# Moving preparation work earlier in a linear-attention layer with a routed feed-forward, and swapping two GpSimd operations

## The chip, the cores and the metric

The kernel runs on one core of one Trainium2 chip. The metric is the device time of one execution in microseconds. Engines are called TensorE (PE in the rows), VectorE (DVE), ScalarE (ACT), GpSimd (POOL) and SyncE (SP, which issues the DMAs).

## The reference

One transformer layer on 8192 tokens of width 512, float32. The six modulation vectors sa, ca, ga, sb, cb, gb come from `silu(c) @ wmod`; ga and gb are kept away from zero.

```python
h = layernorm(x) * (1 + ca) + sa
q, k = elu(h @ Wq.T + bq) + 1, elu(h @ Wk.T + bk) + 1     # 16 heads of 32
v = h @ Wv.T + bv
KV = sum over tokens of k (x) v;  Z = 1 / (q . sum(k) + 1e-6)
x = x + ga * ((q @ KV * Z) @ Wo.T + bo)
h = layernorm(x) * (1 + cb) + sb
V = h @ fWv.T + fbv                                        # value mix
s = ln(V @ Wg.T + bg) + sigmoid(alpha) * ln(norms of the probes Wp @ V)
w = softmax of the two best of 8 experts
x = x + gb * (V + sum over experts of w_e * (silu(V @ W1_e.T + b1_e) @ W2_e.T + b2_e))
```

## The kernel before

The work has two phases with one pass over the tokens each. The first is `sweep_tiles` over T = 64 tiles of 128 tokens. A tile i is normalised (xn), turned (xT), multiplied by Wk and Wq; k of the tile is multiplied with xn into four PSUM banks that gather over all tiles (the sum over tokens), and q goes to DRAM. The second phase is `sweep_pairs` over 32 pairs of tiles, and reads q back. Between them a few products build the matrix G from the sums.

Every matmul operand is split in a high and a low part (`_hi`, `_lo`, float32r), and `three` (L1471) makes three products of them: 12 matmuls of 128x512 for each of the three products of a tile, 36 in a step. In TensorE's step i (L1578) stand k(i), the product of k(i-1) with xn(i-1), and q(i). Each waits for what the other engines made: k(i) for xT_hi from ScalarE (L774), its last third for xT_lo from VectorE (L970); the second product for k_lo from VectorE and xn_lo from GpSimd.

VectorE's step i (L1180) runs in this order: zq of the tile before (L1184, tile qf in the rows), statistics of tile i+2 (L940 to L948), in steps 1 to 16 one `modulation` (L1191), qf (L1195), zk (L1201), xn of tile i+2 (L958), the turn of tile i+1 (L964), kf (L1213, tile zk in the rows), xT_lo (L970), k_lo (L1221). `modulation(v, b)` multiplies one quarter of a 512x512 block of wmod by silu(c) and adds it into row v of mod2; v = 0 to 3 are ga, sb, cb, gb, four steps each. L1044 is the first quarter of each, L1047 the three others.

GpSimd's step i (L656): rstd of tile i+2 (L662), xn_lo of tile i+1 (L667, behind ScalarE's xn_hi, L780), and ks_acc (L672), which adds kf of tile i to the sum of k.

All weights are prepared on the chip, and this work is laid between the tiles by the table `PREP` (L50): step to two lists of jobs, the first run in front of xn of the step (on TensorE behind the k product), the second at the step's end. `prepare` (L1085 on VectorE, L1540 on TensorE, L753 on ScalarE) and `scaled` (L1062) run them. The jobs: bq; sb, gb, ga (TensorE sums a row of mod2 over the partitions, L1492 or L1504; for ga and gb ScalarE copies it to wtmp and VectorE makes the gate of it by `gate`, L1052; ga also multiplies bo_ga, L1113); cat0 to cat3 (VectorE turns a quarter of the router and expert weights and adds it into acc_c, L1097 to L1108); fv, u, bc, bfv, w2 (the products of the value mix with them); v, bv, o (attention's value and output weights). Semaphores keep them in order, and every engine meets the jobs in program order, so that a job that takes long on VectorE delays the tile work behind it.

Of the kernel before, what the change touches and what calls it, by code (L numbers as in the profile page):

```python
# [23 lines left out]
ALU = mybir.AluOpType  # L24
# [7 lines left out]
KB = D // P  # L32
# [14 lines left out]

PREP = {0: ["bq", ""], 13: ["sb", ""], 17: ["gb", ""], 19: ["", "cat0"], 20: ["", "cat1"], 21: ["", "cat2"],  # L50
# [4 lines left out]
PREP_STEPS = 57  # L55
MOD2_LOADS = {-1: 0, 1: 1, 6: 2, 9: 3}


def f32(ap):

    return ap.bitcast(F32)


def wait_count(eng, sem, n):

    if not isinstance(n, int) or n > 0:
        eng.wait_ge(sem, n)
# [14 lines left out]
def prep_job(i, n):  # L82

    return [j for j in PREP.get(i, [])[n:n + 1] if j]


def live(t, tiles):

    return not isinstance(t, int) or 0 <= t < tiles
# [7 lines left out]
def landed(t, slot):  # L97

    return (t - slot) * 8 + 16
# [12 lines left out]
def build(nc, x, Wq, bq, Wk, bk, Wv, bv, Wo, bo, fWv, fbv, Wg, bg, Wp, alpha, g_r, b_r, g_c, b_c,  # L112
          W1, b1, W2, b2, c, wmod, out):
    T = x.shape[1] // P
    assert T % 2 == 0 and T > PREP_STEPS
    J = T // 2
# [9 lines left out]
    with ctx:  # L126
        def sb(name, shape, dt=F32, stack=ctx):
            return stack.enter_context(nc.sbuf_tensor(name, shape, dt))

        def sem(name):  # L130
            return ctx.enter_context(nc.semaphore(name))
# [16 lines left out]
        ks_acc = sb("ks_acc", [P, D])  # L148
# [62 lines left out]
        kf = zk  # L211
# [121 lines left out]
        kf_done = sem("kf_done")  # L333
        kh_done = sem("kh_done")
        kl_done = sem("kl_done")
        ks_done = sem("ks_done")
# [94 lines left out]

        for step_jobs in PREP.values():
            JOBS += [j for j in step_jobs if j and j[0] != "v" and j[:3] != "cat"]
# [6 lines left out]

        SUMMED = {j: n for n, j in enumerate([j for step_jobs in PREP.values() for j in step_jobs
                                              if j[:3] == "cat" or j[:2] == "fv" or j[:1] in ("u", "v")])}

        W_TURNS = {j: n for n, j in enumerate([j for step_jobs in PREP.values() for j in step_jobs
                                               if j[:3] == "cat" or j[:2] == "w2" or j[:1] in ("o", "v")])}
# [41 lines left out]
        def quarters(row):  # L487

            return row.rearrange("p (j i d) -> p i j d", i=KB, j=KB)

        def natural(row):

            return row.rearrange("p (i j d) -> p i j d", i=KB, j=KB)
# [139 lines left out]
        def _(pool):  # L633
# [22 lines left out]
            def step(i, s):  # L656
                if -1 <= i <= 0:
                    pool.wait_ge(xn_done, i + 2)
                    nc.gpsimd.tensor_copy(quarters(xq[:, 1 - s, :]), natural(xn[:, 1 - s, :])).then_inc(xp_done, 1)
                if live(i + 2, T):  # L660
                    wait_count(pool, veps_done, i + 3)
                    nc.gpsimd.tensor_tensor(rstd[:, s:s + 1], veps[:, s:s + 1], neg_half[:, 0:1],  # L662
                                            ALU.pow).then_inc(rstd_done, 1)
                if live(i + 1, T):
                    pool.wait_ge(xnh_done, i + 2)
                    pool.wait_ge(xn_done, i + 2)
                    nc.gpsimd.tensor_tensor(quarters(xn_lo[:, 1 - s, :]), natural(xn[:, 1 - s, :]),  # L667
                                            quarters(f32(xn_hi[:, 1 - s, :])), ALU.subtract).then_inc(xnl_done, 1)
                if live(i, T):
                    pool.wait_ge(kf_done, i + 1)  # L670
                    wait_count(pool, ks_done, i)
                    nc.gpsimd.tensor_tensor(ks_acc[:], ks_acc[:], kf[:, s, :], ALU.add).then_inc(ks_done, 1)  # L672

            sweep_tiles(step, -2, T - 1)

            def biased_x(j):
# [247 lines left out]
        def _(dve):  # L924
# [13 lines left out]
            def statistics(i, s):  # L938
                dve.wait_ge(x_in[s], landed(i, s))
                nc.vector.bn_stats(stats[:, s, :], xin[:, s, :]).then_inc(stats_done, 1)  # L940
                dve.wait_ge(stats_done, i + 1)

            def mean_var(i, s):
                nc.vector.bn_aggr(mv[:, s, :], stats[:, s, :]).then_inc(mv_done, 1)

            def var_eps(i, s):
                dve.wait_ge(mv_done, i + 1)
                nc.vector.tensor_scalar(veps[:, s:s + 1], mv[:, s, 1:2], EPS, None, ALU.add).then_inc(veps_done, 1)  # L948
# [89 lines left out]
            ga, gb = mod2[:, GA, :], mod2[:, GB, :]  # L1038

            def modulation(v, b):  # L1040

                dve.wait_ge(wmv_in[v], 16)
                if b == 0:
                    ins = nc.vector.tensor_scalar(mod2[:, v, :], wm_in[:, v % 2, b, :], c_col[:, 2, b:b + 1], None, ALU.mult)  # L1044
                else:
                    dve.wait_ge(mod2_done, KB * v + b)
                    ins = nc.vector.scalar_tensor_tensor(out=mod2[:, v, :], in0=wm_in[:, v % 2, b, :],  # L1047
                                                         scalar=c_col[:, 2, b:b + 1], in1=mod2[:, v, :],
                                                         op0=ALU.mult, op1=ALU.add)
                ins.then_inc(mod2_done, 1)  # L1050
# [129 lines left out]
            def step(i, s):  # L1180
                if live(i - 1, T):
                    dve.wait_ge(q_psum, i)
                    wait_count(dve, q_out[1 - s], landed(i - 1, 1 - s) - 16)
                    nc.vector.tensor_tensor(zq[:, 1 - s, :], bank_q, bq_row[:], ALU.add).then_inc(zq_done, 1)  # L1184
                early_turn = i == 0
                ahead = live(i + 2, T)
                if ahead:
                    statistics(i + 2, s)
                    mean_var(i + 2, s)
                    var_eps(i + 2, s)  # L1190
                if 1 <= i <= 4 * KB:  # L1191
                    modulation((i - 1) // KB, (i - 1) % KB)
                if live(i - 1, T):
                    dve.wait_ge(eq_done, i)
                    nc.vector.scalar_tensor_tensor(out=qf[:, 1 - s, :], in0=zq[:, 1 - s, :], scalar=0.0,  # L1195
                                                   in1=exp_q[:, 1 - s, :], op0=ALU.max, op1=ALU.add).then_inc(qf_done, 1)
                if live(i, T):
                    dve.wait_ge(k_psum, i + 1)
                    wait_count(dve, kh_done, i - 1)
                    wait_count(dve, ks_done, i - 1)  # L1200
                    nc.vector.tensor_tensor(zk[:, s, :], bank_k, bk_row[:], ALU.add).then_inc(zk_done, 1)  # L1201
                if early_turn:
                    for b in range(KB):
                        low_q(b)
                    xT_low(i + 1, 1 - s)
                prepare(i, 0)
                if ahead:
                    normed(i + 2, s)
                if live(i + 1, T) and not early_turn:
                    turned_x(i + 1, 1 - s)  # L1210
                if live(i, T):
                    dve.wait_ge(ek_done, i + 1)
                    nc.vector.scalar_tensor_tensor(out=kf[:, s, :], in0=zk[:, s, :], scalar=0.0,  # L1213
                                                   in1=exp_k[:, s, :], op0=ALU.max, op1=ALU.add).then_inc(kf_done, 1)
                    scaled(i)
                    if live(i + 1, T) and not early_turn:
                        xT_low(i + 1, 1 - s)
                    dve.wait_ge(kf_done, i + 1)
                    dve.wait_ge(kh_done, i + 1)
                    wait_count(dve, m_done, i - 1)  # L1220
                    nc.vector.tensor_tensor(k_lo[:, s, :], kf[:, s, :], f32(k_hi[:, s, :]), ALU.subtract).then_inc(kl_done, 1)  # L1221
                prepare(i, 1)
                if i == 15:
                    bias_columns()
                if i == 35:
                    b2_and_value_bias()
                if isinstance(i, int) and i == PREP_STEPS - 1:
                    router_constants()

            sweep_tiles(step, 0, T)  # L1230


# [512 lines left out]
```

## Time and profile before

| | us |
|---|---|
| median of 3 runs | 1271.91 (1270.49 to 1272.03) |
| profiled execution | 1271.91 |
| its span, first to last instruction | 1270.2 |
| PE busy | 1224.7 (96%) |
| DVE busy | 997.0 (78%) |
| ACT busy | 538.0 (42%) |
| POOL busy | 547.8 (43%) |

Times in rows count from the start of the span. Busy time of an engine is the time in which an instruction of it runs, and an instruction that is held up by something inside the machine counts as running. TensorE's matmuls overlap: one of 128x512 is shown with 0.39 us and the next starts 0.23 us later. The table of the program's groups calls a tile by its name in the kernel without the buffer's number, so mod2 appears as mod and the gathered sums as ps.

### The profile page before, as it was taken

The page shows a single profiled execution, that of the slowest core. Times are in us where ns is not written, and L with a number is a line of the kernel's source. Part 1 is how long each engine was busy: PE and PEld are TensorE (multiplying, and loading weights), DVE is VectorE, ACT ScalarE, POOL GpSimd, SP SyncE. Part 2 cuts the span into 40 slices and gives each one's busy share as a digit, 9 for nine tenths or more (in the row PEclk, how much of TensorE's full clock was granted, in tenths as well). Part 3 has the DMA queues.
Part 4 walks back from the last instruction along what each step waited for, and adds up shares of the span by engine and source line. Part 5 has one row for each costly group of instructions (what it writes and reads, how often), then busy time and mean ns, then how long its engine had stood idle before and what let it go on. Part 6 is the DMA issues. An engine that isn't in the chain of part 4 may idle for free.

```text
span 1270.2 us, 18483 instructions
## 1 busy us (share of the span) xinstructions
PE 1224.7 (96%) x5742; PEld 999.4 (79%) x5742; DVE 997.0 (78%) x2275; ACT 538.0 (42%) x1117; POOL 547.8 (43%) x401
## 2 busy tenths in 40 slices
PE   8999999999999999998789999999999999999998
PEld 5788878788777788885678888788887888888887
DVE  5887788888889888877578777777877777778764
ACT  2454454545445554443334343433434334343431
POOL 1434433333334433433346464554645445364531
PEclk9999999999999999999899999999999999999999
DMA  8455534444334443432322221313223131322201
GB/s 214 157 174 178 162 122 144 145 137 126 108 105 127 133 133 108 125 116 75 83 67 67 84 92 58 100 55 96 73 78 99 51 100 59 92 84 66 84 17 51
DMA packets 131681, 131.64 MB, mean 104 GB/s; under 512 B 12328, under 2 KB 86480, under 8 KB 131584
## 3 DMA queue, kind: packets, MB, share of 16 engines
q1 hardware_dynamic: 131584, 130.47, 33.8%
q8 instruction: 46, 0.75, 0.3%
q14 instruction: 51, 0.42, 0.1%
HBM read 80.62 MB, written 49.81 MB: 103 GB/s over the span
## 4 chain that ended last, share of the span: by engine, by line
PE 65%; DVE 11%; POOL 11%; issue 6%; ACT 4%; DMA 1%; SPq 0%; POOLq 0%; DVEq 0%; ACTq 0%
PE ps L1475 20%; PE ps L1476 20%; PE ps L1480 20%; POOL xb L679 6%; POOL rrs L718 3%; PE ps L1662 2%; POOL rstd L711 2%; DVE x L1303 2%; DVE xT_lo L1310 1%; DVE marked L1393 1%; PE ps L1568 1%; ACT xn L879 1%; DVE zk L1201 1%; DMA wm_in<-in_L_wmod_dram 1%; DVE m L1386 1%
## 5 line engine op out<-in xcount | busy, mean ns | idle before, releaser
L705 POOL TENSOR_TENSOR cn<-c,half 128x16 f32<-128x16 f32 x32 | 104.2, 3257 | 281.5 <-DVE c L1338 281.5
L667 POOL TENSOR_TENSOR xn_lo<-xn,xn_hi 128x512 fp32r<-128x512 f32 x64 | 85.5, 1337 | 278.1 <-ACT xn_hi L780 278.1
L1475 PE MATMUL ps<-g_hi,qT_hi 128*128 128x512 f32 x256 | 104.8, 410 | 4.9 <-ACT qT_hi L843 4.9
L798 ACT ACTIVATE exp_q<-qf 128x512 f32<-128x512 f32 x64 | 40.5, 632 | 156.7 <-DVE qf L1184 156.7
L1475 PE MATMUL ps<-wk_hi,xT_hi 128*128 128x512 f32 x256 | 102.0, 398 | 2.4 <-ACT xT_hi L774 2.4
L1475 PE MATMUL ps<-wq_hi,xT_hi 128*128 128x512 f32 x256 | 102.4, 400 | 0.5 <-DVE wq_lo L1006 0.5
L1475 PE MATMUL ps<-v_hi,xT_hi 128*128 128x512 f32 x256 | 102.9, 402 | 0.0
L1475 PE MATMUL ps<-k_hi,xn_hi 128*128 128x512 f32 x256 | 102.3, 400 | 0.0
L1476 PE MATMUL ps<-g_lo,qT_hi 128*128 128x512 f32 x256 | 101.8, 398 | 0.0
L1476 PE MATMUL ps<-wq_lo,xT_hi 128*128 128x512 f32 x256 | 101.4, 396 | 0.0
L1476 PE MATMUL ps<-wk_lo,xT_hi 128*128 128x512 f32 x256 | 101.3, 396 | 0.0
L1476 PE MATMUL ps<-k_lo,xn_hi 128*128 128x512 f32 x256 | 100.7, 393 | 0.0
L1476 PE MATMUL ps<-v_lo,xT_hi 128*128 128x512 f32 x256 | 100.2, 391 | 0.0
L1480 PE MATMUL ps<-k_hi,xn_lo 128*128 128x512 f32 x256 | 100.1, 391 | 0.0
L836 ACT CAST xT_hi<-ps 128x512 fp32r<-128x512 f32 x64 | 37.5, 587 | 131.9 <-PE ps L1662 131.9
L672 POOL TENSOR_TENSOR ks_acc<-ks_acc,zk 128x512 f32<-128x512 f32 x64 | 88.0, 1376 | 4.6 <-DVE zk L1213 4.6
L679 POOL TENSOR_TENSOR xb<-xin,bo_ga 128x1024 f32<-128x1024 f32 x32 | 77.8, 2431 | 9.5 <-DMA xin<-_attn_hidden_states_dram 9.3
L1475 PE MATMUL ps<-c_hi,xT_hi 128*128 128x328 f32 x256 | 80.7, 324 | 0.0
L697 POOL TENSOR_TENSOR qks<-q_in,ks_q 128x1024 f32<-128x1024 f32 x32 | 76.9, 2403 | 8.4 <-DMA q_in<-q_scratch 8.4
L1476 PE MATMUL ps<-c_lo,xT_hi 128*128 128x328 f32 x256 | 77.9, 315 | 0.0
L805 ACT ACTIVATE exp_k<-zk 128x512 f32<-128x512 f32 x64 | 40.6, 634 | 87.9 <-DVE zk L1201 87.8
L662 POOL TENSOR_TENSOR rstd<-veps,neg_half 128x1 f32<-128x1 f32 x64 | 44.7, 698 | 73.5 <-DVE veps L948 72.7
(240 smaller groups left out, 3292.5 us busy)
## 6 DMA issues: line engine op xcount, KB each, us to landing
xin<-_attn_hidden_states_dram SPq DMA_DIRECT2D x64, 256.0 KB, 3.1
q_scratch<-qf SPq DMA_DIRECT2D x64, 256.0 KB, 3.3
xin<-_attn_hidden_states_dram SPq DMA_DIRECT2D x32, 512.0 KB, 4.1
q_in<-q_scratch SPq DMA_DIRECT2D x128, 128.0 KB, 2.9
out_dram<-qf SPq DMA_DIRECT2D x64, 256.0 KB, 2.0
xn_scratch<-xn SPq DMA_DIRECT2D x62, 256.0 KB, 2.1
xq<-xn_scratch SPq DMA_DIRECT2D x248, 64.0 KB, 2.4
wm_in<-in_L_wmod_dram SPq DMA_DIRECT2D x4, 1024.0 KB, 5.6
```

Of the source, the lines that this page charges most:

```text
L662: nc.gpsimd.tensor_tensor(rstd[:, s:s + 1], veps[:, s:s + 1], neg_half[:, 0:1], ALU.pow).then_inc(rstd_done, 1)
L667: nc.gpsimd.tensor_tensor(quarters(xn_lo[:, 1 - s, :]), natural(xn[:, 1 - s, :]), quarters(f32(xn_hi[:, 1 - s, :])), ALU.subtract).then_in ...
L672: nc.gpsimd.tensor_tensor(ks_acc[:], ks_acc[:], kf[:, s, :], ALU.add).then_inc(ks_done, 1)
L679: nc.gpsimd.tensor_tensor(xb[:], xin[:], bo_ga[:].unsqueeze(1).to_broadcast([P, 2, D]), ALU.add).then_inc(xb_done, 1)
L697: nc.gpsimd.tensor_tensor(qks[:].rearrange("p h (g f) -> p (h g) f", f=P), q_of(j).rearrange("p (n f) -> p n f", f=P), ks_q[:].unsqueeze(1 ...
L705: nc.gpsimd.tensor_tensor(cn[:].rearrange("p h e -> p (h e)"), c2[:].rearrange("p h e -> p (h e)"), half[:], ALU.pow).then_inc(cn_done, 1)
L718: nc.gpsimd.tensor_tensor(rrs[:].rearrange("p h k -> p (h k)"), rve[:], neg_half[:, 0:4], ALU.pow).then_inc(rrs_done, 1)
L798: nc.scalar.activation(exp_q[:, 1 - s, :], zq[:, 1 - s, :], ACT.Relu, scale=-1.0).then_inc(rq_done, 1)
L805: nc.scalar.activation(exp_k[:, s, :], zk[:, s, :], ACT.Relu, scale=-1.0).then_inc(rk_done, 1)
L1475: nc.tensor.matmul(dst, ah, bh, start=start and n == 0, stop=False)
L1476: nc.tensor.matmul(dst, ah, bl, start=False, stop=False)
L1480: last = nc.tensor.matmul(dst, al_, bh, start=False, stop=stop and n == len(parts) - 1)
```

## The change

Three things are changed. The `PREP` table puts ga at step 6 instead of 50, the jobs cat0 to cat3 two steps earlier (17 to 20, with gb at 18 instead of 17), and all that follows two to five steps earlier; `router_constants` thereby runs at step 51 instead of 56, and `b2_and_value_bias` at 24 instead of 35. On VectorE the `modulation` of steps 1 to 16 stands behind k_lo instead of behind the statistics. On GpSimd ks_acc(i) stands ahead of xn_lo(i+1).

```diff
-PREP = {0: ["bq", ""], 13: ["sb", ""], 17: ["gb", ""], 19: ["", "cat0"], 20: ["", "cat1"], 21: ["", "cat2"],
-        22: ["", "cat3"], 24: ["", "fv0"], 25: ["u0", ""], 27: ["", "fv1"], ...
+PREP = {0: ["bq", ""], 6: ["", "ga"], 13: ["sb", ""], 17: ["", "cat0"], 18: ["gb", "cat1"], 19: ["", "cat2"],
+        20: ["", "cat3"], 22: ["", "fv0"], 23: ["u0", ""], 25: ["", "fv1"], ...
...
@@ GpSimd
+                if live(i, T):
+                    pool.wait_ge(kf_done, i + 1)
+                    wait_count(pool, ks_done, i)
+                    nc.gpsimd.tensor_tensor(ks_acc[:], ks_acc[:], kf[:, s, :], ALU.add).then_inc(ks_done, 1)
                 if live(i + 1, T):
                     pool.wait_ge(xnh_done, i + 2)
                     pool.wait_ge(xn_done, i + 2)
                     nc.gpsimd.tensor_tensor(quarters(xn_lo[:, 1 - s, :]), natural(xn[:, 1 - s, :]),
                                             quarters(f32(xn_hi[:, 1 - s, :])), ALU.subtract).then_inc(xnl_done, 1)
-                if live(i, T):
-                    pool.wait_ge(kf_done, i + 1)
-                    wait_count(pool, ks_done, i)
-                    nc.gpsimd.tensor_tensor(ks_acc[:], ks_acc[:], kf[:, s, :], ALU.add).then_inc(ks_done, 1)
@@ VectorE
                     var_eps(i + 2, s)
-                if 1 <= i <= 4 * KB:
-                    modulation((i - 1) // KB, (i - 1) % KB)
                 if live(i - 1, T):
...
                     nc.vector.tensor_tensor(k_lo[:, s, :], kf[:, s, :], f32(k_hi[:, s, :]), ALU.subtract).then_inc(kl_done, 1)
+                if 1 <= i <= 4 * KB:
+                    modulation((i - 1) // KB, (i - 1) % KB)
                 prepare(i, 1)
                 if i == 15:
                     bias_columns()
-                if i == 35:
+                if i == 24:
                     b2_and_value_bias()
```

The order on the engines shows the change at three places. In the changed kernel kf, k_lo, qf and zk have the lines L1211, L1219, L1193 and L1199, and ks_acc and xn_lo on GpSimd L667 and L671.

GpSimd before, at the first tiles: xq is a copy for the first two tiles alone.

```order
L662 TENSOR_TENSOR rstd<-veps,neg_half 128x1
L667 TENSOR_TENSOR xn_lo<-xn,xn_hi 128x4x4x32
L672 TENSOR_TENSOR ks_acc<-ks_acc,zk 128x512
L662 TENSOR_TENSOR rstd<-veps,neg_half 128x1
L667 TENSOR_TENSOR xn_lo<-xn,xn_hi 128x4x4x32
```

GpSimd of the changed kernel, at the same place.

```order
L662 TENSOR_TENSOR rstd<-veps,neg_half 128x1
L667 TENSOR_TENSOR ks_acc<-ks_acc,zk 128x512
L671 TENSOR_TENSOR xn_lo<-xn,xn_hi 128x4x4x32
L662 TENSOR_TENSOR rstd<-veps,neg_half 128x1
L667 TENSOR_TENSOR ks_acc<-ks_acc,zk 128x512
```

The two operations have changed places in each step.

VectorE before, step 6, from veps to the first operation of step 7: mod is the modulation's accumulator.

```order
L948 TENSOR_SCALAR veps<-mv 128x1
L1047 SCALAR_TENSOR_TENSOR mod<-wm_in,c_col,mod 128x512
L1195 SCALAR_TENSOR_TENSOR qf<-qf,exp_q 128x512
L1201 TENSOR_TENSOR zk<-ps,bk_row 128x512
L958 TENSOR_SCALAR xn<-xin,mv,rstd 128x512
L964 STREAM_TRANSPOSE ps<-xq 128x4x4x32
L1213 SCALAR_TENSOR_TENSOR zk<-zk,exp_k 128x512
L970 TENSOR_TENSOR xT_lo<-ps,xT_hi 128x512
L1221 TENSOR_TENSOR k_lo<-zk,k_hi 128x512
L1184 TENSOR_TENSOR qf<-ps,bq_row 128x512
```

VectorE of the changed kernel, step 6 from xn on, again to the first operation of step 7.

```order
L958 TENSOR_SCALAR xn<-xin,mv,rstd 128x512
L964 STREAM_TRANSPOSE ps<-xq 128x4x4x32
L1211 SCALAR_TENSOR_TENSOR zk<-zk,exp_k 128x512
L970 TENSOR_TENSOR xT_lo<-ps,xT_hi 128x512
L1219 TENSOR_TENSOR k_lo<-zk,k_hi 128x512
L1047 SCALAR_TENSOR_TENSOR mod<-wm_in,c_col,mod 128x512
L1056 TENSOR_SCALAR wtmp<-wtmp 128x512
L1057 TENSOR_SCALAR wtmp<-wtmp 128x512
L1058 TENSOR_TENSOR wtmp<-wtmp 128x512
L1059 SCALAR_TENSOR_TENSOR mod<-wtmp 128x512
L1113 TENSOR_TENSOR bo_ga<-bo_ga,mod 128x512
L1184 TENSOR_TENSOR qf<-ps,bq_row 128x512
```

The modulation has moved from the front to behind k_lo, and the five operations of the gate ga have come in behind it.

VectorE of the changed kernel, step 18, from zk to the middle of cat1. Before, the four operations of the gate stood at this place of step 17, and no job stood behind k_lo in steps 17 and 18.

```order
L1199 TENSOR_TENSOR zk<-ps,bk_row 128x512
L1056 TENSOR_SCALAR wtmp<-wtmp 128x512
L1057 TENSOR_SCALAR wtmp<-wtmp 128x512
L1058 TENSOR_TENSOR wtmp<-wtmp 128x512
L1059 SCALAR_TENSOR_TENSOR mod<-wtmp 128x512
L958 TENSOR_SCALAR xn<-xin,mv,rstd 128x512
L964 STREAM_TRANSPOSE ps<-xq 128x4x4x32
L1211 SCALAR_TENSOR_TENSOR zk<-zk,exp_k 128x512
L970 TENSOR_TENSOR xT_lo<-ps,xT_hi 128x512
L1219 TENSOR_TENSOR k_lo<-zk,k_hi 128x512
L1100 STREAM_TRANSPOSE catT<-raw_cat 128x352
L1103 TENSOR_REDUCE small<-catT 128x1
```

Gate and cat job now stand in one step, with cat0 in the step ahead of it and cat2 and cat3 in the two behind.

## Rows read from the trace of the kernel before

**Rows 1.** The page: span, and busy time of TensorE with its share and instructions.
```profile
span 1270.2 us, 18483 instructions
PE 1224.7 (96%) x5742; PEld 999.4 (79%) x5742; DVE 997.0 (78%) x2275; ACT 538.0 (42%) x1117; POOL 547.8 (43%) x401
```
**Rows 2.** Chain of waits in order of time: start us, us, what.
```profile
62.24 0.93 PE ps L1480 x4
70.61 0.93 PE ps L1480 x4
```
**Rows 3.** Waits of TensorE's weight loads, first phase: us in total, times, longest.
```profile
PEld ps L1475 <- ACT xT_hi L774: 4.7, 6, 1.3
```
**Rows 4.** Timeline, first matmul of steps: start, us, what [idle before <-releaser].
```profile
216.23 0.39 PE L1475 MATMUL ps<-wk_hi,xT_hi 128*128 128x512 f32 x1
...
225.05 0.50 PE L1475 MATMUL ps<-wk_hi,xT_hi 128*128 128x512 f32 x1 [0.29 <-ACT xT_hi L774]
...
234.54 0.50 PE L1475 MATMUL ps<-wk_hi,xT_hi 128*128 128x512 f32 x1 [0.89 <-ACT xT_hi L774]
...
372.03 0.39 PE L1475 MATMUL ps<-wk_hi,xT_hi 128*128 128x512 f32 x1
...
424.18 0.39 PE L1475 MATMUL ps<-wk_hi,xT_hi 128*128 128x512 f32 x1
```
**Rows 5.** Timeline, VectorE from one L1184 to the next around cat2, and GpSimd.
```profile
210.33 0.68 DVE L1184 TENSOR_TENSOR qf<-ps,bq_row 128x512 f32<-128x512 f32 x1
...
215.03 0.69 DVE L1213 SCALAR_TENSOR_TENSOR zk<-zk,exp_k 128x512 f32<-128x512 f32 x1 [0.27 <-ACT exp_k L807]
...
216.47 0.69 DVE L1221 TENSOR_TENSOR k_lo<-zk,k_hi 128x512 fp32r<-128x512 f32 x1
...
218.39 1.55 DVE L997 SCALAR_TENSOR_TENSOR acc_c<-catT,col_turn,acc_c 128x328 f32<-128x328 f32 x1
219.86 0.68 DVE L1184 TENSOR_TENSOR qf<-ps,bq_row 128x512 f32<-128x512 f32 x1
...
218.28 1.29 POOL L672 TENSOR_TENSOR ks_acc<-ks_acc,zk 128x512 f32<-128x512 f32 x1
```
**Rows 6.** Timeline, VectorE and GpSimd in the last tile.
```profile
581.56 0.69 DVE L1213 SCALAR_TENSOR_TENSOR zk<-zk,exp_k 128x512 f32<-128x512 f32 x1 [1.36 <-ACT exp_k L807]
583.00 1.18 DVE L1221 TENSOR_TENSOR k_lo<-zk,k_hi 128x512 fp32r<-128x512 f32 x1 [0.74 <-ACT k_hi L813]
...
582.33 1.29 POOL L672 TENSOR_TENSOR ks_acc<-ks_acc,zk 128x512 f32<-128x512 f32 x1 [4.61 <-DVE zk L1213]
```
**Rows 7.** Timeline, GpSimd and VectorE in step 27.
```profile
269.36 1.30 POOL L667 TENSOR_TENSOR xn_lo<-xn,xn_hi 128x512 fp32r<-128x512 f32 x1 [4.47 <-ACT xn_hi L780]
270.61 1.74 POOL L672 TENSOR_TENSOR ks_acc<-ks_acc,zk 128x512 f32<-128x512 f32 x1
...
269.83 1.37 DVE L1221 TENSOR_TENSOR k_lo<-zk,k_hi 128x512 fp32r<-128x512 f32 x1
271.13 1.78 DVE L1081 TENSOR_TENSOR v_lo<-wtmp,v_hi 128x512 fp32r<-128x512 f32 x1
```
**Rows 8.** The modulation's two lines: count, ns min/median/max, first and last start.
```profile
L1044 DVE TENSOR_SCALAR mod<-wm_in,c_col x4: 479/479/1164, 40.3 to 140.1; 128x512 f32<-128x512 f32 x4
...
L1047 DVE SCALAR_TENSOR_TENSOR mod<-wm_in,c_col,mod x12: 751/752/1043, 48.1 to 167.1; 128x512 f32<-128x512 f32 x12
```
**Rows 9.** Timeline, VectorE: gate gb in step 17, bo_ga in step 50.
```profile
178.00 0.43 DVE L1056 TENSOR_SCALAR wtmp<-wtmp 128x512 f32<-128x512 f32 x1 [0.79 <-ACT wtmp L759]
...
180.38 0.55 DVE L958 TENSOR_SCALAR xn<-xin,mv,rstd 128x512 f32<-128x512 f32 x1
...
478.46 0.69 DVE L1113 TENSOR_TENSOR bo_ga<-bo_ga,mod 128x512 f32<-128x512 f32 x1
```
**Rows 10.** TensorE's line L1504 (job sb): count, ns, first and last start.
```profile
L1504 PE MATMUL ps<-ones,mod x16: 166/250/250, 141.1 to 142.7; 128*128 128x1 f32 x16
```
**Rows 11.** Sums of a stretch: busy time of each engine, granted clock, DMA.
```profile
603.00:610.00 7.00, 3.83 (x9) 3.08 (x10) 6.90 (x8) 1.33 (x3) 1.33 (x1) 0.55 0.50 150
```

More of the change, by code:

```diff
@@ L46 @@
 TAKEN = -3.3e38
-PREP = {0: ["bq", ""], 13: ["sb", ""], 17: ["gb", ""], 19: ["", "cat0"], 20: ["", "cat1"], 21: ["", "cat2"],
[4 rows of a table removed]
-PREP_STEPS = 57
+PREP = {0: ["bq", ""], 6: ["", "ga"], 13: ["sb", ""], 17: ["", "cat0"], 18: ["gb", "cat1"], 19: ["", "cat2"],
[4 rows of a table added]
+PREP_STEPS = 52
 MOD2_LOADS = {-1: 0, 1: 1, 6: 2, 9: 3}
```

8 rows, old and new, of the table PREP are left out of this document.

## The prediction

> **What bounds the kernel now.** I read the page first, then the chain of waits, what TensorE waits for, and last the rows of VectorE, GpSimd and TensorE beside each other. TensorE is busy 96% of the span [rows 1]. In the first phase (64 tiles) its chain repeats the same block of L1480 every 8.37 us [rows 2]: that is 36 matmuls of one tile back to back, and no step can be shorter. So an edit of this phase pays or costs only by how long TensorE is left without input. It waits for one thing there: xT_hi, six times, 4.7 us of its weight loads [rows 3]. The first wk_hi matmul of steps 22, 24, 39 and 45 starts at 216.23, 234.54, 372.03 and 424.18 [rows 4]. Two steps take 18.31 instead of 16.74 (1.57 lost), six take 52.15 instead of 50.22 (1.93 lost). That is 3.5 us of stall in the whole phase, and more is not to be had by moving this work.
>
> Why xT_hi is late: VectorE falls behind. Call lag the time from TensorE's start of a step to VectorE's L1184 in it. L1184 at 219.86 [rows 5] and TensorE's next start at 225.05, ended by xT_hi [rows 4], are 5.19 apart. So TensorE's step lasts 8.37 plus its own extra work, or lag + 5.19 if that is longer: the limit is a lag of 3.18. Lag grows by VectorE's own period minus TensorE's step, and can't fall under about 0.34.
>
> VectorE's period is where the change acts. In the cat step L1184 follows L1184 after 9.53 us (210.33, 219.86) [rows 5]. The last piece is L997, 1.55 us for 328 columns, which ends 0.37 after GpSimd's ks_acc (218.28 + 1.29). That is a block, not work: VectorE waits while GpSimd's instruction runs.
>
> **Who blocks whom.** Two places show it in full. In the last tile, where no xn_lo comes first, ks_acc starts 0.08 after kf (581.56 + 0.69) and k_lo, issued at 583.00, takes 1.18, ending 0.55 after ks_acc [rows 6]. In step 27 three turns follow each other: GpSimd xn_lo 269.36 to 270.66, VectorE k_lo until 271.20, GpSimd ks_acc stretched to 1.74 until 272.35, VectorE v_lo until 272.91 [rows 7]. When both have an instruction waiting, they alternate. From GpSimd's first start to the end of VectorE's second blocked instruction it is 3.55 us.
>
> The Trainium skill (SBUF — State Buffer, section "Who interferes with whom") has the rule that speaks against this change: an instruction of VectorE with two SBUF inputs and one of GpSimd that reads SBUF exclude each other for the whole instruction, and who starts first goes first. The trace agrees, with 1.18 for k_lo; the rule says nothing of the order when both queue, for which rows 7 stand. If the two only shared bandwidth, k_lo would be stretched in part and the forecast would come out near the first rival.
>
> **The swap on GpSimd.** Every tile: before, ks_acc came after xn_lo, so k_lo was issued before GpSimd had anything running. Now ks_acc starts at kf + 0.08, and k_lo, issued 0.7 later, waits. From rows 5, kf ends 5.39 after L1184 (215.72 - 210.33). So k_lo ends at 5.39 + 0.08 + 1.29 + 0.55 = 7.31, where it ended at 6.83 (216.47 + 0.69), and the next L1184 starts 0.08 earlier than that end. Ordinary period when lagging: 7.23 instead of 6.75. Cost 0.48 per step; hidden below 8.37, but lag is worked off more slowly. In return GpSimd's pair is over at 5.39 + 0.08 + 3.0 = 8.47 (3.0 from GpSimd's two instructions of [rows 7]), so a cat step ends its last piece at about 9.0 instead of 9.53: four times 0.5 gained. v_lo, w_lo and b2st gain likewise, mostly in steps that TensorE covers anyway.
>
> **The modulations.** Sixteen of them (four L1044, twelve L1047), steps 1 to 16, move from behind veps to behind k_lo. At the old place most took 0.48 and 0.75 [rows 8], part of it in the time in which VectorE waited for exp_q anyway. At the new place GpSimd's xn_lo stands in the queue when k_lo ends, takes the turn, and the modulation is the second blocked instruction of the pattern of rows 7. Period: 5.39 + 0.08 + 3.55 - 0.07 = 8.95 for L1047, and 8.68 for L1044 (0.27 shorter). Both are over 8.37. The bounds of one such step: 7.23 + 0.67 = 7.90 if it takes the pair before xn_lo, 8.95 by the nearest rows, 9.2 if GpSimd kept the pair for both of its instructions. I take 8.95, since rows 7 have this very queue.
>
> **The gate ga, step 50 to 6.** The TensorE sum costs the same (0.85 of its own work in the step) at either place. On VectorE four instructions take 2.38 (178.00 to 180.38) and bo_ga 0.73 [rows 9], 3.11 in all, 3.2 with the wait between. At step 50 it was hidden; now it lands on steps with no slack.
>
> **The sum, steps 1 to 16.** VectorE: 12 x 8.95 + 4 x 8.68 + 3.2 (gate) + 0.35 (sb_col, cb1_col) + 0.48 (bias_columns) = 146.1. TensorE without stall: 16 x 8.37 + 0.85 (ga) + 1.75 (sb: its 16 narrow matmuls, the last at 1.6 behind the first [rows 10]) = 136.5. The lag at step 1 is 1.3 (before it was 0.8, and k_lo is 0.5 later) and at step 17 it stands at 8.95 - 5.19 = 3.76, so 2.5 of the difference are absorbed. Stall: 146.1 - 136.5 - 2.5 = 7.1 us, from step 5 on, with the largest piece in step 7, behind the gate. The last modulation of step 12 is also awaited by sb in step 13: about 1.1 us, part of the 7.1.
>
> **Steps 17 to 21** (cat0, gb + cat1, cat2, cat3, nothing). VectorE 8.85 + 11.4 + 9.0 + 9.0 + 7.23 = 45.5, where 11.4 is 9.0 and the gate's 2.4. TensorE 5 x 8.37 + 0.86 (gb) = 42.7. Lag goes from 3.76 to 7.23 - 5.19 = 2.04, which gives back 1.7 as stall: 45.5 - 42.7 + 1.7 = 4.5 us. Before, the same four cat steps cost 1.7, as they began with no lag and gb stood two steps ahead of them.
>
> **Steps 22 to 63.** fv and u: TensorE's own transposes and matmuls in these steps cover VectorE, before as after. bfv behind bc: VectorE about 12.3 against 9.21, lag 3.45, stall 0.3 (0.7 before). w2: period 9.2 instead of 10.5, lag at most 2.9, none (1.2 before). v: 9.0 instead of 8.4, for acc_v now meets xn_lo; lag climbs to 3.7 at step 45, where bv's 0.9 on TensorE covers it. Stall here 0.3.
>
> Total stall 7.1 + 4.5 + 0.3 = 11.9, less the 3.5 of before: +8.4. Executions: the span was 1270.2 [rows 1] and the profiled time 1271.91, so 1.7 lie around it, and that time is also the median of the runs shown. The second phase runs the same instructions and I give it nothing. **1271.9 + 8.4 = 1280.3 us.**
>
> **Rivals.**
> 1. VectorE keeps the pair. If L1047 gets in directly after k_lo, its period is 7.90, steps 1 to 16 have no lag but for the gate, and the cats start from nearly none: lag 0.8, 3.0, 3.6, 3.8 and a stall of 1.4 in all. 1271.9 - 3.5 + 1.4 = 1269.8; with the gate of step 6 blocked once, near 1271. For it: the earlier end of GpSimd's pair, seen as 1.5 us in L997. Against it: ks_acc's 1.74 and v_lo's 1.78 in rows 7, which alternate. It decides at a period of 8.37.
> 2. GpSimd keeps the pair for both of its instructions. Then k_lo ends at 8.6 and even an ordinary step takes 8.5, over 8.37: another 4 us in steps 1 to 16 and 4 or more behind. About 1288. Against it: k_lo got in between xn_lo and ks_acc in rows 7.
> 3. TensorE's clock falls in the holes. Behind a hole of 3 us between the phases the granted clock is 0.55 over 603 to 610 [rows 11], that is mostly the level of 1.2 GHz. The hole of step 7, 3.3 us in two pieces, is the largest here. Some eight microseconds of matmuls at half speed would add 4 us, so 1284. Against it: the stalls of 0.3 and 0.9 in rows 4 left the clock at full speed. The Trainium skill (TensorE: Matmul & The Clock Gate, "What's actually happening") says that the clock follows how busy the array has lately been; here the holes after step 7 are 0.6 in 9, so I don't expect it.
>
> **How the numbers follow.** Forecast 0.74, its own range 1277 to 1283.5 (a period of 8.8 to 9.1 for the modulation steps is 2.4 us either way). Rival 1: 0.13, most of it faster, some within the bound. Rival 2: 0.04. Rival 3: 0.09. A measurement of this kernel can tell about 0.2% (2.5 us) from no change; the three runs lie within 1.5 us. So faster 0.09, same 0.08, slower 0.83. The range is 1275 to 1285: it leaves out most of rival 1 and rival 2.
>
> **What would show it.** Right: k_lo about 1.2 us in nearly all of 64 tiles; the modulations 1.7 or more, each ending 0.55 behind xn_lo; xn_lo stretched to 1.74; TensorE waiting for xT_hi in steps 5 to 12 by 0.3 to 0.6 and in step 7 by over 3; L1184 to L1184 8.95 there; L997 at about 0.5. Wrong: modulations of 0.75 behind k_lo, or steps 8 to 12 at 8.37; or a granted clock under 1.00 between 80 and 260 us, which would be rival 3.

## The result and the profile after

| | before | changed |
|---|---|---|
| median, us | 1271.97 (4 runs) | 1280.55 (4 runs, 1279.32 to 1280.94) |
| profiled execution | 1271.91 | 1278.65 |
| its span | 1270.2 | 1276.9 |

The ratio is 1.0064 with a 95% interval of 1.0052 to 1.0078, so the changed kernel is slower, clear of the noise: by 8.6 us between the two medians above, by 8.1 us by the ratio, which takes in more executions than these four. A later series of the same kernel gave 1280.39 and 1.0068 (1.0056 to 1.0081).

First the steps of the first phase, as [rows 4] show them for before. Timeline of TensorE in the changed kernel, first wk_hi matmul of steps 1, 7, 8, 9, 10, 17, 22 and 63 (start us, us, what, idle before and what ended it):

```profile
38.07 0.40 PE L1475 MATMUL ps<-wk_hi,xT_hi 128*128 128x512 f32 x1
...
89.36 0.39 PE L1475 MATMUL ps<-wk_hi,xT_hi 128*128 128x512 f32 x1
...
100.76 0.51 PE L1475 MATMUL ps<-wk_hi,xT_hi 128*128 128x512 f32 x1 [1.39 <-ACT xT_hi L774]
...
109.70 0.50 PE L1475 MATMUL ps<-wk_hi,xT_hi 128*128 128x512 f32 x1 [0.33 <-ACT xT_hi L774]
...
118.64 0.50 PE L1475 MATMUL ps<-wk_hi,xT_hi 128*128 128x512 f32 x1 [0.32 <-ACT xT_hi L774]
...
181.64 0.39 PE L1475 MATMUL ps<-wk_hi,xT_hi 128*128 128x512 f32 x1
...
227.96 0.50 PE L1475 MATMUL ps<-wk_hi,xT_hi 128*128 128x512 f32 x1 [0.39 <-ACT xT_hi L774]
...
584.45 0.39 PE L1475 MATMUL ps<-wk_hi,xT_hi 128*128 128x512 f32 x1
```

Timeline of TensorE in the kernel before, the first wk_hi matmul of steps 1, 17 and 63 (that of 22 is in [rows 4]):

```profile
37.93 0.39 PE L1475 MATMUL ps<-wk_hi,xT_hi 128*128 128x512 f32 x1
...
173.53 0.39 PE L1475 MATMUL ps<-wk_hi,xT_hi 128*128 128x512 f32 x1
...
576.51 0.39 PE L1475 MATMUL ps<-wk_hi,xT_hi 128*128 128x512 f32 x1
```

| stretch | before | changed | difference | forecast |
|---|---|---|---|---|
| steps 1 to 16 | 135.60 | 143.57 | +7.97, of it 0.85 the sum of ga and 7.1 stall | 7.1 stall |
| steps 17 to 21 | 42.70 | 46.32 | +3.6 stall | 4.5 |
| steps 22 to 62 | 360.28 | 356.49 | -3.79, of it -0.85 ga and -2.9 stall | -3.2 |
| together | 538.58 | 546.38 | +7.8 | +8.4 |

In the table, stall is the time that TensorE stood without input, and ga the 0.85 us of its own work that moved with the gate. The last column is the prediction's. Steps 8 and 9 last 8.94 each (100.76, 109.70, 118.64), where a step of before takes 8.37 [rows 2], and step 7 takes 11.40.

Waits of TensorE's weight loads in the first phase of the changed kernel (us in total, times, longest); before it was 4.7 us in six waits [rows 3]:

```profile
PEld ps L1475 <- ACT xT_hi L774: 10.8, 13, 2.1
PEld ps L1475 <- DVE qf L1184: 1.6, 1, 1.6
```

The second row is a wait that before did not have: q of step 7 needs its PSUM bank, and VectorE frees it with L1184, late behind the gate.

Then the cause. Timeline of VectorE and of GpSimd in step 10 of the changed kernel (L1211 is kf, L1219 k_lo, GpSimd's L667 ks_acc, L671 xn_lo):

```profile
126.84 0.69 DVE L1211 SCALAR_TENSOR_TENSOR zk<-zk,exp_k 128x512 f32<-128x512 f32 x1 [0.27 <-ACT exp_k L807]
127.45 0.69 DVE L970 TENSOR_TENSOR xT_lo<-ps,xT_hi 128x512 fp32r<-128x512 f32 x1
128.28 1.17 DVE L1219 TENSOR_TENSOR k_lo<-zk,k_hi 128x512 fp32r<-128x512 f32 x1
129.38 1.78 DVE L1047 SCALAR_TENSOR_TENSOR mod<-wm_in,c_col,mod 128x512 f32<-128x512 f32 x1
131.08 0.68 DVE L1184 TENSOR_TENSOR qf<-ps,bq_row 128x512 f32<-128x512 f32 x1
...
127.61 1.29 POOL L667 TENSOR_TENSOR ks_acc<-ks_acc,zk 128x512 f32<-128x512 f32 x1 [3.15 <-DVE zk L1211]
128.86 1.75 POOL L671 TENSOR_TENSOR xn_lo<-xn,xn_hi 128x512 fp32r<-128x512 f32 x1
```

This is the queue of [rows 7] with other names: ks_acc until 128.90, k_lo until 129.45, xn_lo until 130.61, the modulation until 131.16. Each of the two VectorE instructions ends 0.55 behind the GpSimd instruction that blocked it. xT_lo, with one input in PSUM, runs 0.69 beside ks_acc. All instances of the lines (count, ns min/median/max, first and last start) in the changed kernel; [rows 8] showed the modulations at 479 and 752:

```profile
L1047 DVE SCALAR_TENSOR_TENSOR mod<-wm_in,c_col,mod x12: 1767/1776/1782, 55.3 to 183.2; 128x512 f32<-128x512 f32 x12
...
L1044 DVE TENSOR_SCALAR mod<-wm_in,c_col x4: 1509/1514/1519, 46.6 to 156.2; 128x512 f32<-128x512 f32 x4
...
L1219 DVE TENSOR_TENSOR k_lo<-zk,k_hi x64: 743/1184/1455, 38.3 to 590.9; 128x512 fp32r<-128x512 f32 x64
...
L671 POOL TENSOR_TENSOR xn_lo<-xn,xn_hi x64: 1267/1745/1767, 18.1 to 583.2; 128x512 fp32r<-128x512 f32 x64
```

Not one of the sixteen modulations escapes the queue, and nearly every k_lo is stretched (1.18 in the middle of 64).

### The profile page after: what moved, and what is told of

The parts are those of the page before. It is cut to its first block, busy times and chain, and to the rows that moved or that the text cites. A ratio compares the mean times of both kernels' runs of the same rounds, so it can differ in the third digit from the quotient of the medians.

```text
span 1276.9 us, 18483 instructions
## 1 busy us (share of the span) xinstructions
PE 1225.7 (96%) x5742; PEld 997.7 (78%) x5742; DVE 1025.5 (80%) x2275; ACT 537.6 (42%) x1117; POOL 558.1 (44%) x401
## 4 chain that ended last, share of the span: by engine, by line
PE 58%; DVE 15%; POOL 11%; issue 7%; ACT 7%; DMA 1%; SPq 0%; DVEq 0%; POOLq 0%; ACTq 0%
PE ps L1475 18%; PE ps L1476 18%; PE ps L1480 17%; POOL xb L679 6%; POOL rrs L718 3%; PE ps L1662 2%; POOL rstd L711 2%; DVE x L1303 2%; DVE mod L1047 2%; DVE xT_lo L1310 1%; DVE zk L1199 1%; DVE zk L1211 1%; DVE qf L1184 1%; ACT exp_k L805 1%; ACT exp_q L798 1%
## 5 line engine op out<-in xcount | busy, mean ns | idle before, releaser
L667 POOL TENSOR_TENSOR ks_acc<-ks_acc,zk 128x512 f32<-128x512 f32 x64 | 83.1, 1299 | 219.1 <-DVE zk L1211 219.1
L671 POOL TENSOR_TENSOR xn_lo<-xn,xn_hi 128x512 fp32r<-128x512 f32 x64 | 109.6, 1712 | 0.0
L662 POOL TENSOR_TENSOR rstd<-veps,neg_half 128x1 f32<-128x1 f32 x64 | 35.3, 551 | 135.3 <-DVE veps L948 135.3
L1219 DVE TENSOR_TENSOR k_lo<-zk,k_hi 128x512 fp32r<-128x512 f32 x64 | 75.6, 1182 | 8.5 <-ACT k_hi L813 1.7
```

## The experiments

The whole time of an execution also varies in stretches that no edit touches (see the last section), so for each kernel the length of the first phase, from the start of step 1 to that of step 63, stands beside the median. That length is from the one profiled execution. The ratios are against executions of the kernel before on the same chip in the same series, with medians of 1271.56 (e1 to e4), 1271.42 (e5 to e7) and 1271.17 (e8, e9).

| kernel | table | modulation | GpSimd | first phase | median | ratio, 95% interval |
|---|---|---|---|---|---|---|
| before | old | front | xn_lo first | 538.6 | 1271.97 | |
| changed | new | behind k_lo | ks_acc first | 546.4 | 1280.55 | 1.0064 (1.0052 to 1.0078) |
| e1 | new | front | ks_acc first | 536.8 | 1271.49 | 0.9995 (0.9987 to 1.0004) |
| e2 | new | behind k_lo | xn_lo first | 542.9 | 1278.28 | 1.0053 (1.0040 to 1.0067) |
| e3 | new | front | xn_lo first | 540.2 | 1274.79 | 1.0026 (1.0018 to 1.0035) |
| e4 | old | front | ks_acc first | 535.8 | 1269.02 | 0.9979 (0.9970 to 0.9987) |
| e5 | old | behind k_lo | xn_lo first | 538.6 | 1271.34 | 0.9995 (0.9984 to 1.0006) |
| e6 | new | behind k_lo | ks_acc, then memset | 536.0 | 1270.29 | 0.9987 (0.9977 to 0.9997) |
| e7 | new, ga at 46 | behind k_lo | ks_acc first | 547.9 | 1280.96 | 1.0073 (1.0052 to 1.0093) |
| e8 | new, sb at 14 | behind k_lo | ks_acc first | 546.4 | 1279.79 | 1.0067 (1.0053 to 1.0080) |
| e9 | the changed kernel again | | | 547.3 | 1280.39 | 1.0068 (1.0056 to 1.0081) |

Against the medians of before, the first phase accounts for the whole time to within 0.8 us in the changed kernel, e4, e5, e7, e8 and e9. The medians of e1, e2, e3 and e6 are 1.5 to 2.4 us higher than their first phase would make them. Why is not shown.

The single edits and their sum are worth a look. In the first phase the table alone costs 1.6 (e3), the modulations' place alone nothing (e5), and GpSimd's order alone gives back 2.8 (e4); together they cost 7.8. The old table with both new orders was not run.

**e1: the modulations back in front.**

```diff
                     var_eps(i + 2, s)
+                if 1 <= i <= 4 * KB:
+                    modulation((i - 1) // KB, (i - 1) % KB)
...
-                if 1 <= i <= 4 * KB:
-                    modulation((i - 1) // KB, (i - 1) % KB)
                 prepare(i, 1)
```

> The changed kernel with the modulations of steps 1 to 16 back behind the statistics; the table and GpSimd's new order stay. Theory of the turns (VectorE's second blocked instruction behind k_lo makes a step 8.95 long): the modulation is now outside the queue, a modulation step is under 7.7 on VectorE, TensorE loses nothing in steps 8 to 13, step 7 has no stall (lag 0.3 + 11 - 9.2 = 2.1, limit 3.18), the cats start from no lag and stall 1.1 in steps 20 and 21, bfv 0.3. Stall of the first phase about 1.5 instead of 11.3, so the time is 1270 to 1271, 2 below the kernel before. Rival (the table's density costs the time: ga on step 6, gb beside cat1): the stalls of steps 7 and 18 stay, about 5 us, and the time is 1276 or more.

The first phase shrinks by 9.6 us to 536.8, 1.8 under before: steps 1 to 16 take 136.47 (before plus the 0.85 of ga), step 7 has 8.37, and steps 17 to 21 take 43.82, with the 1.1 expected. The rival is refuted. The median fell by 9.1, to that of before on the same chip (1271.56); the 2 us under it that were expected are not in the medians. They are in the profiles, 1269.87 against 1271.91, but e1's profiled execution is the fastest of its eleven. The modulation in front takes 0.75 in all twelve:

```profile
L1047 DVE SCALAR_TENSOR_TENSOR mod<-wm_in,c_col,mod x12: 750/751/753, 46.7 to 166.5; 128x512 f32<-128x512 f32 x12
```

**e2: GpSimd's old order.**

```diff
-                if live(i, T):
-                    nc.gpsimd.tensor_tensor(ks_acc[:], ks_acc[:], kf[:, s, :], ALU.add).then_inc(ks_done, 1)
                 if live(i + 1, T):
...
+                if live(i, T):
+                    nc.gpsimd.tensor_tensor(ks_acc[:], ks_acc[:], kf[:, s, :], ALU.add).then_inc(ks_done, 1)
```

> The changed kernel with GpSimd's old order (xn_lo, then ks_acc); table and modulations behind k_lo stay. Theory of the turns: k_lo is issued before xn_lo and takes 0.69, the modulation is blocked once, by xn_lo alone, and VectorE's modulation step is 8.45 instead of 8.95, so TensorE loses 0.1 per step in 8 to 12. But each cat step is 9.5 again (L997 at 1.55 behind ks_acc) and the ordinary one 7.0, so steps 17 to 21 stall about 5 and w2 and bfv about 2.5. About 1277 to 1279. Rival (GpSimd's swap alone is the harm, by k_lo at 1.18 in each tile): the time falls to about 1272.

The median of 1278.28 is within the expected range, but 2.4 us of its distance from before lie outside the first phase. The modulation step on VectorE is 8.45 (L1184 to L1184), steps 8 to 12 of TensorE last 8.36 to 8.47, steps 1 to 16 138.59. Cats and gate cost 3.7 in steps 17 to 21, where about 5 was expected, and w2 stalls again as before. Step 7 still loses 1.3. The modulation of step 6 is blocked behind xn_lo, and with GpSimd's old order the first instruction of the gate is blocked behind ks_acc (1.51, where it takes 0.41 in the changed kernel):

```profile
87.56 1.78 DVE L1047 SCALAR_TENSOR_TENSOR mod<-wm_in,c_col,mod 128x512 f32<-128x512 f32 x1
89.27 1.51 DVE L1056 TENSOR_SCALAR wtmp<-wtmp 128x512 f32<-128x512 f32 x1
...
87.47 1.33 POOL L667 TENSOR_TENSOR xn_lo<-xn,xn_hi 128x512 fp32r<-128x512 f32 x1 [4.33 <-ACT xn_hi L780]
88.77 1.73 POOL L672 TENSOR_TENSOR ks_acc<-ks_acc,zk 128x512 f32<-128x512 f32 x1
```

**e3: the table alone.** Both edits of e1 and e2.

> The new table alone: modulations in front and GpSimd's old order. Theory of the turns: steps 1 to 16 as before but for the gate behind step 6, 12.1 on VectorE, lag 3.2 against a limit of 3.2, no more than 0.3 of stall; cats of 9.5 beside the gate gb stall 4.5 in steps 18 to 22, bfv and w2 about 2.9. About 1275 to 1276. Rival (the table is neutral): 1272.

The median of 1274.79 is just under the expected range. The stalls were smaller than expected: steps 1 to 16 lose 0.4, steps 17 to 21 2.7 (45.41) where 4.5 was expected for cats and gate, and w2 behind bfv stalls again. So the new table alone costs 1.6 us in the first phase, and by the medians twice that: gate gb and cat1 in one step, and w20 and w21 packed nearer to bfv.

**e4: GpSimd's order alone, on the kernel before.**

```diff
+                if live(i, T):
+                    nc.gpsimd.tensor_tensor(ks_acc[:], ks_acc[:], kf[:, s, :], ALU.add).then_inc(ks_done, 1)
                 if live(i + 1, T):
...
-                if live(i, T):
-                    nc.gpsimd.tensor_tensor(ks_acc[:], ks_acc[:], kf[:, s, :], ALU.add).then_inc(ks_done, 1)
```

> The kernel before with GpSimd's new order alone. Theory of the turns: k_lo takes 1.18 in every tile, yet no ordinary step is over 8.37 on VectorE (7.25), a modulation step is about 7.6; a cat step falls from 9.5 to 9.0 and four of them from no lag reach 2.9, under the limit of 3.18: the stall of 1.6 in steps 22 to 24 goes. bfv stalls 0.3 instead of 0.7, w2 and v nothing instead of 1.2. Stall of the phase about 0.3 instead of 3.5: 1268.8, faster by 0.25%. Rival (the swap harms, since k_lo is stretched 64 times): slower than 1272.

The best version: 1269.02, faster than before by 0.2%, with the whole interval under 1. The first phase falls by 2.8 us, though k_lo is stretched in nearly every tile; the cat jobs' L997 takes 0.56 where it took 1.55 in [rows 5], and TensorE waits for xT_hi 1.4 us instead of 4.7. All instances of k_lo and of L997's cat jobs, then TensorE's wait, in e4:

```profile
L1221 DVE TENSOR_TENSOR k_lo<-zk,k_hi x64: 758/1183/1469, 38.2 to 580.3; 128x512 fp32r<-128x512 f32 x64
```
```profile
L997 DVE SCALAR_TENSOR_TENSOR acc_c<-catT,col_turn,acc_c x3: 559/560/560, 208.9 to 227.0; 128x328 f32<-128x328 f32 x3
```
```profile
PEld ps L1475 <- ACT xT_hi L774: 1.4, 3, 0.7
```

**e5: the modulations' place alone, on the kernel before.** The edit of e1 the other way round, on before.

> The kernel before with the modulations alone moved behind k_lo. Theory of the turns: GpSimd still runs xn_lo first, so k_lo takes 0.69 and the modulation is blocked once: VectorE's modulation step is 8.45, lag grows by 0.08 a step to about 1.3 and is absorbed. Steps 1 to 17 take the 135.6 us of before, all later stalls stay at 3.5: no change, within 0.5 us of 1271.6. Rival (the new place of the modulations costs by itself): 3 to 7 us slower.

No change, as expected: steps 1 to 16 take 135.60 to the hundredth. Yet the modulations are as long as in the changed kernel:

```profile
L1047 DVE SCALAR_TENSOR_TENSOR mod<-wm_in,c_col,mod x12: 1774/1784/1799, 54.1 to 173.0; 128x512 f32<-128x512 f32 x12
```

Here k_lo is not blocked, so VectorE's step is 8.45 instead of 8.95, and 0.08 a step is absorbed by the lag. It takes both blocks in one step to pass 8.37 by enough.

**e6: GpSimd's second instruction only writes.**

```diff
-                    nc.gpsimd.tensor_tensor(quarters(xn_lo[:, 1 - s, :]), natural(xn[:, 1 - s, :]),
-                                            quarters(f32(xn_hi[:, 1 - s, :])), ALU.subtract).then_inc(xnl_done, 1)
+                    nc.gpsimd.memset(f32(xn_lo[:, 1 - s, :]), 0.0).then_inc(xnl_done, 1)
```

> The changed kernel with GpSimd's xn_lo made by a memset to zero in place of the subtraction, so the low part of xn is left out of the sums. GpSimd's instruction of this place then only writes. If two readers of SBUF exclude each other and a writer does not (theory), L1047 takes 0.75 behind k_lo instead of 1.78 while k_lo still takes 1.18 behind ks_acc; a modulation step is 7.9 and steps 1 to 17 take about 136.5 us, with the whole at 1270 to 1271. L1044, with a single SBUF tensor, tells whether the writer blocks that kind. Rival (any instruction of GpSimd blocks): L1047 stays blocked for as long as the memset runs, and the step is between 8.2 and 8.9.

The order is that of the changed kernel, and k_lo still queues behind ks_acc, but 10.4 us of the first phase are gone. The low part of xn is left out of the sums. Timeline of VectorE and GpSimd in step 10 of e6 (its lines are one lower; L1218 is k_lo, L1046 the modulation):

```profile
119.68 1.18 DVE L1218 TENSOR_TENSOR k_lo<-zk,k_hi 128x512 fp32r<-128x512 f32 x1
120.78 0.74 DVE L1046 SCALAR_TENSOR_TENSOR mod<-wm_in,c_col,mod 128x512 f32<-128x512 f32 x1
...
119.01 1.30 POOL L667 TENSOR_TENSOR ks_acc<-ks_acc,zk 128x512 f32<-128x512 f32 x1 [3.15 <-DVE zk L1210]
120.25 0.53 POOL L671 MEMSET xn_lo<- 128x512 f32 x1
```

k_lo waits for ks_acc as before. The memset runs its 0.53 while k_lo runs, where the subtraction was held until k_lo's end (1.75). So here a GpSimd instruction that only writes was not held up by VectorE's two SBUF inputs. The memset is over when the modulation starts, so whether it could block one, L1044's kind above all, is not shown.

**e7: ga late.**

```diff
-PREP = {0: ["bq", ""], 6: ["", "ga"], 13: ["sb", ""], ...
+PREP = {0: ["bq", ""], 13: ["sb", ""], ...
...
+        45: ["", "bv"], 46: ["", "ga"], ...
```

> The changed kernel with ga at the end of step 46 instead of step 6. Theory: VectorE's sum of steps 1 to 16 falls by the gate's 3.08, TensorE's own work there by 0.85, so the stall there falls by 2.2 and steps 1 to 17 take 140.5 us instead of 143.6; steps 8 to 12 still last 8.94. At 46 the gate brings the lag to 2.8, and the o steps behind it stall 0.7 to 1. In all about 1.4 less: 1279. Rival (the gate is the cause of most of the loss): 1275.

Steps 7 to 12 behave as the theory has it: 8.95, 8.94, 8.93, 8.67, 8.94, 8.95, and no stall of 3 us. But steps 1 to 16 take 142.0 instead of 140.5, all of it in step 13 (12.93 instead of 11.33), and steps 47 to 53 lose 2.8, where 0.7 to 1 was expected: the gate left a lag of 3.84 instead of 2.8, and the o steps, 8.73 each on VectorE, never work it off. So 1279 was missed as well as the rival's 1275: the time was no better than the changed kernel's. What happened in step 13 led to e8 and e9. The granted clock there was 0.61, in a stretch's sums (us, busy time and count of PE, PEld, DVE, ACT, POOL, then the clock, DMA share and GB/s):

```profile
148.00:151.00 3.00, 3.00 (x10) 2.31 (x9) 2.96 (x7) 1.77 (x3) 0.08 (x1) 0.61 0.20 76
```

**e8: sb one step later.** `13: ["sb", ""]` becomes `14: ["sb", ""]` in the changed kernel's table.

> The changed kernel with sb at step 14 instead of 13, so that TensorE need not wait for the modulation of step 12 in front of the 16 narrow matmuls. Theory of the turns: VectorE's sum is the same, step 13 lasts 8.9 instead of 11.3 and step 14 10.1 instead of 8.4, the lag at step 17 is 3.8 instead of 3.3, so steps 1 to 17 take 143.1 instead of 143.6 us. If TensorE's clock falls behind the hole at this place in many executions of the changed kernel (second theory, from the profile without the early gate, granted clock 0.61 over 148 to 151), the median falls by more, up to 2 us, to 1278.6. If not, it stays within 0.6 of 1280.5.

Steps 1 to 16 take 143.07, the wait in front of L1504 is gone, and the clock stays at 1.00 there. VectorE enters step 17 with a lag of 3.74 instead of 3.27, and steps 17 to 21 stall 4.1 instead of 3.6, so the first phase is as long as before this edit (546.4). The median is 1279.79 against 1280.39 of e9, the changed kernel once more, on the same chip. The two ranges overlap (1279.36 to 1280.85, 1278.70 to 1280.93), so a gain in whole time is not shown, and the larger one that was expected if the clock fell in many executions did not come.

**e9: the changed kernel again.**

> The changed kernel once more, for the spread of its executions and a second profile. The first phase should again take 546.4 us between the starts of steps 1 and 63, or 548 if the clock falls behind the wait in step 13; the median 1280.5. If profiles differ outside this phase, by 1 to 2 us in the stretch around the products between the phases, then the difference between the profiled 1278.65 and the median is chance of that stretch.

Its profile has a step 13 of 12.92 us, where the first profile had 11.33. TensorE's narrow matmuls of sb and the products behind them in e9:

```profile
148.80 1.95 PE L1504 MATMUL ps<-ones,mod 128*128 128x1 f32 x16 [0.82 <-DVE mod L1047]
...
151.15 0.39 PE L1480 MATMUL ps<-k_hi,xn_lo 128*128 128x512 f32 x1
...
151.64 0.63 PE L1476 MATMUL ps<-k_lo,xn_hi 128*128 128x512 f32 x1
```

And the sums of the 3 us behind, first e9, then the same stretch in the first profile of the changed kernel:

```profile
151.00:154.00 3.00, 3.00 (x10) 2.37 (x9) 2.96 (x7) 1.84 (x3) 0.00 (x0) 0.60 0.23 87
```
```profile
151.00:154.00 3.00, 3.00 (x15) 2.45 (x15) 2.96 (x7) 1.59 (x3) 0.27 (x1) 1.00 0.16 61
```

Ten matmuls instead of fifteen in 3 us: the clock stood mostly at 1.2 GHz. The fall follows the wait of 0.8 us and 16 matmuls of one column each; over 154 to 158 the granted clock was 0.88.

## Why the prediction was right, point by point

- **Only TensorE's hunger counts, limit lag + 5.19.** Right. In the changed kernel the lag settles at 3.75 and steps 8 to 12 take 8.94 each, but 8.69 in step 10, behind the one L1044 among them. The least lag is 0.20, not 0.34; no term of the sum uses it.
- **The swap costs k_lo 0.48 in each tile, hidden.** Right, and e4 shows the hidden cost beside what it brings: k_lo at 1.18, and yet 2.8 us less in the first phase.
- **The modulation becomes the second blocked instruction, 8.95 and 8.68.** Right to 0.01: 129.38 + 1.78 above. e1, e5 and e6 take away the new place, the swap with the table, and GpSimd's reads; each frees steps 1 to 16. Neither of the two order changes does it alone on the old table (e4, e5); on the new table GpSimd's swap alone costs nothing there (e1), the modulations' place alone 2.1 (e2), of which 0.4 is there without it (e3).
- **The gate ga, 3.2.** Measured 12.03 - 8.95 = 3.08 on VectorE. Stall in step 7: 3.0 against over 3, but not all of it for xT_hi, as the prediction had it: 1.2 was TensorE idle for the PSUM bank that L1184 frees, and 1.4 for xT_hi.
- **Steps 1 to 16: 7.1.** Measured 7.1, but two errors of about 0.5 cancel in it. VectorE's sum was 145.6 for 146.1, as the 0.35 for sb_col and cb1_col did not show (step 13 took 8.66) and the gate was shorter; and the lag grew by 2.0 for 2.5, to 3.27 at step 17.
- **Steps 17 to 21: 4.5.** Too large; 3.6 measured. The lag at step 17 was 3.27, not 3.76, since VectorE caught up in step 13, in which TensorE does sb and waits for it (lag 1.08 at step 14). The gate beside cat1 made a step of 11.0 instead of 11.4. With the lag at 3.74 (e8) the stall is 4.1, so the lag and the gate each account for about half of the miss.
- **Steps 22 to 63: 0.3 against 3.5.** Measured about 0.65 against 3.5. I had left out 0.1 to 0.2 in each of steps 22 and 23.
- **The sum.** +7.8 in the profiled first phase for +8.4 forecast. Profiled time against profiled time it is only +6.7, as the stretches around took 1.0 less; median against median 8.6. That the forecast of 1280.3 lies within 0.3 of the median is partly luck: its sum was 0.6 too large, and the profile that it is worked out for turned out 1.9 under the median.
- **Rivals.** Rival 1 (VectorE keeps the pair) and rival 2 (GpSimd keeps it) are refuted by the timeline of step 10. Rival 3 I gave 0.09 and laid into step 7. The clock stayed at full speed there in every profile, but fell in step 13 in two of the three profiles with a wait of 0.8 for sb (e7 and e9, not the first of the changed kernel; e2, with a wait of 0.3, kept it). It costs about 1.6 us in that step, and 0.9 in the first phase (547.29 against 546.38), since VectorE catches up meanwhile. Whether it falls there in most executions is not shown.

## What to carry to other kernels

Before an operation is moved on VectorE, look at what GpSimd has running and waiting at the new place, and count the turns: two VectorE instructions with two SBUF inputs each, one behind the other, with two GpSimd instructions queued that read SBUF, took 3.55 us here for 1.4 us of work. A swap of two GpSimd operations can pay (e4) although it stretches an instruction in each of 64 tiles, if the step has slack and the block leaves a place that has none. An engine that lags shows as a wait of the bound engine only past a limit, so compare periods, not busy shares.

## What the runs showed of the hardware that was not expected

- A GpSimd memset of 128x512 ran 0.53 us beside a VectorE instruction with two SBUF inputs, where a subtraction of the same shape was held for 0.45.
- A hole of 0.8 us in TensorE's work, followed by 16 one-column matmuls (1.95 us), was followed by a granted clock of 0.61 and 0.60 over 3 us in two profiles (e7, e9) and by 1.00 in the first one of the changed kernel. A hole of 1.4 us between full matmuls, in front of step 8, was followed by 1.00 in all three profiles that have it (changed, e8, e9).
- Outside the first phase spans differ without an edit: the head up to step 1 took 36.4 to 38.1 us and the stretch from step 63 to the end 692.5 to 695.7 us in eleven profiles. Both go with the granted clock. Over 22 to 27 us it was 1.00 in four profiles, with heads of 36.4 to 36.9, and 0.66 or 0.67 in seven, with heads of 37.8 to 38.1. Over 585 to 660 us it was 0.93 where the stretch behind took 692.5 to 693.5, 0.91 where it took 693.7 to 695.2, and 0.89 where it took 695.4 and 695.7. A change of 2 us in the first phase can be lost in that.
